# A graph layer on one core: an early small read of the adjacency, and half a tile rounded on VectorE in place of ScalarE

## The reference

```python
h   = maximum(layernorm(x, axis=-1), 0.0)     # (x - mean) / sqrt(var + 1e-5), no gain or offset
agg = matmul(adj, h)
out = x + relu(matmul(agg, W.T) + b)
```

## Time and profile before

| | |
|---|---|
| median of 3 runs | 381.19 us |
| the profiled execution's own time | 380.8 us |
| its span (first to last instruction) | 379.0 us |
| PE busy | 375.1 us (99%) |
| PE matmuls of the adjacency (L421) | 1536, each 389 ns on average, overlapping |
| DVE busy | 212.2 us (56%) |
| ACT busy | 181.8 us (48%) |
| POOL busy | 50.1 us (13%) |

### The profile page before, as it was taken

The page is one execution under the profiler, slowest core; times in us unless marked ns, Lnnn a source line. Parts: engine busy times, 40 slices in busy tenths (PEclk is TensorE's granted clock), DMA queues, the critical chain, the costliest instruction groups (busy, mean ns, idle before and its releaser), DMA issues.

```text
span 379.0 us, 4516 instructions
## 1 busy us (share of the span) xinstructions
PE 375.1 (99%) x1651; PEld 308.1 (81%) x1651; DVE 212.2 (56%) x294; ACT 181.8 (48%) x228; POOL 50.1 (13%) x88
## 2 busy tenths in 40 slices
PE   8999999999999999999999999999999999999997
PEld 4888888888888888888888888888888888888885
DVE  5999988874744453535564544444464444444424
ACT  5888776764443434343643343433355243434341
POOL 5687732320010000000001000000000100000000
PEclk9999999999999999999999999999999999999999
DMA  7989877577659565655566856565656775555203
GB/s 263 369 301 304 275 256 258 185 235 256 210 186 317 174 215 178 208 177 209 176 206 207 294 178 209 178 205 184 201 189 195 256 242 195 187 202 185 92 2 111
DMA packets 22774, 80.25 MB, mean 212 GB/s; under 512 B 2496, under 2 KB 2880, under 8 KB 22752
## 3 DMA queue, kind: packets, MB, share of 16 engines
q1 hardware_dynamic: 19584, 68.30, 54.1%
q0 software_dynamic: 3168, 11.67, 8.6%
HBM read 75.76 MB, written 4.19 MB: 211 GB/s over the span
## 4 chain that ended last, share of the span: by engine, by line
PE 98%; DMA 1%; DVE 0%; ACT 0%; POOL 0%; issue 0%; POOLq 0%
PE bank L421 92%; PE bank L463 6%; DMA x_sb<-x_dram 1%; ACT adj_hi L346 0%; POOL rstd L204 0%; ACT h_sb L352 0%; DVE out_sb L320 0%; DVE stats L240 0%; DVE mean_var L245 0%; DVE var_eps L249 0%; POOLq L200 0%
## 5 line engine op out<-in xcount | busy, mean ns | idle before, releaser
L421 PE MATMUL bank<-adj_hi,h_sb 128*128 128x512 f32 x1024 | 254.3, 389 | 0.2 <-ACT adj_hi L346 0.2
L229 DVE TENSOR_TENSOR adj_lo<-adj_in,adj_hi 128x1024 fp32r<-128x1024 f32 x126 | 154.6, 1227 | 145.7 <-ACT adj_hi L342 145.5
L421 PEld LDWEIGHTS bank<-adj_hi,h_sb 128*128 128x128 f32 x1024 | 192.0, 188 | 40.5 <-issue 0.5
L342 ACT ACTIVATE adj_hi<-adj_in 128x1024 fp32r<-128x1024 f32 x126 | 133.5, 1060 | 176.7 <-PE bank L421 174.5
L421 PE MATMUL bank<-adj_lo,h_sb 128*128 128x512 f32 x512 | 137.5, 389 | 0.0
L421 PEld LDWEIGHTS bank<-adj_lo,h_sb 128*128 128x128 f32 x512 | 96.1, 188 | 20.0
L204 POOL TENSOR_TENSOR rstd<-var_eps,minus_half 128x1 f32<-128x1 f32 x32 | 30.5, 954 | 3.4 <-DVE var_eps L249 0.8
L221 POOL DMA_DIRECT2D out_t_dram<-out_sb x3 | 2.2, 726 | 211.0 <-DVE out_sb L320 211.0
L352 ACT ACTIVATE h_sb<-centred,rstd 128x256 fp32r<-128x256 f32 x32 | 16.0, 499 | 3.6 <-POOL rstd L204 3.2
L362 ACT ACTIVATE centred<-x_sb,neg_mean 128x256 f32<-128x256 f32 x31 | 15.5, 500 | 2.1 <-DVE neg_mean L264 1.9
L270 DVE SCALAR_TENSOR_TENSOR h_sb<-centred,rstd,h_sb 128x256 fp32r<-128x256 f32 x32 | 15.3, 477 | 1.0 <-ACT h_sb L352 1.0
(11 more groups left out here) (25 smaller groups left out, 42.7 us busy)
## 6 DMA issues: line engine op xcount, KB each, us to landing
adj_in<-adj_t_dram SPq DMA_DIRECT2D x126, 512.0 KB, 3.6
xt_sb<-x_t_dram POOLq DMA_DIRECT2D x4, 1024.0 KB, 7.4
x_sb<-x_dram POOLq DMA_DIRECT2D x7, 512.0 KB, 6.5
out_t_dram<-out_sb POOLq DMA_DIRECT2D x3, 1024.0 KB, 4.9
adj_in<-adj_t_dram SPq DMA_DIRECT2D x4, 256.0 KB, 4.8
out_t_dram<-out_sb SPq DMA_DIRECT2D x3, 256.0 KB, 2.0
x_sb<-x_dram POOLq DMA_DIRECT2D x3, 128.0 KB, 4.6
w_sb<-w_t_dram POOLq DMA_DIRECT2D x1, 256.0 KB, 6.0
```

The costliest lines, as they stand in the source:

```text
L229: nc.vector.tensor_tensor(adj_lo[:, k, :], adj_in[:, k, :], adj_hi[:, k, :].bitcast(fp32), ALU.subtract).then_inc(s_lo, 1)
L342: nc.scalar.activation(adj_hi[:, k, :], adj_in[:, k, :], ACT.Copy).then_inc(s_hi, 1)
L421: last = nc.tensor.matmul(bank(g, kb, c)[:], h_sb[:, t, hp, kb * P:(kb + 1) * P], adj_parts[ap][:, n % U, chunk(c)], start=(t == 0 and (hp ...
```

## The change

ScalarE's queue issues, as the very first thing, a DMA of 16 columns of every fourth partition's row of adjacency tile 0 (32 rows of 64 bytes, rows 2 MB apart in memory) into a small tile `touched`, which nobody reads. SyncE waits for its landing only ahead of the last stores. VectorE rounds chunk 0 of tile 0 with a copy, between centre_first and h_rest(0), and waits for that chunk's landing itself. ScalarE no longer does this rounding; it waits until the count of rounded pieces is 1 before it rounds chunk 1. `WARM_ON` goes from 3 to 1.

```diff
-    WARM_ON = 3
+    WARM_ON = 1
...
+    TOUCH = 4
+    TOUCH_COLS = 16
...
+        touched = sb("touched", [P // TOUCH, TOUCH_COLS])
...
+        s_touched = sem("touched_landed")
...
+            sp.wait_ge(s_touched, 16)
             sp.wait_ge(s_out, 16 * LAST)
...
+            def first_rounded():
+
+                dve.wait_ge(s_early[0][0], 16)
+                nc.vector.tensor_copy(adj_hi[:, 0, chunk(0)], adj_in[:, 0, chunk(0)]).then_inc(s_hi, 1)
+
...
             centre_first()
+            first_rounded()
             h_rest(0)
...
+            act.dma_start(touched[:], adj_v[0:P:TOUCH, 0, 0:TOUCH_COLS]).then_inc(s_touched, 16)
+
             nc.scalar.activation(scratch[:], nc.const_aps.tensor(1.0, [P, 1], fp32), ACT.Copy)
             h_rounded(0)
-            early_rounded(0, 0)
+
+            act.wait_ge(s_hi, 1)
             early_rounded(0, 1)
```

## The result

The changed kernel takes 381.55 us (median of 21 runs, 380.89 to 382.84) against 381.1 us of the kernel before beside it (21 runs, 380.58 to 381.66). The ratio is 1.0015 with a 95% interval of 1.0008 to 1.0022: 0.3 to 0.8 us slower, small but real. The runs of the changed kernel also lie wider: four of the 21 stand between 382.75 and 382.84, where the kernel before has none; I call these the far runs. The profiled execution took 381.1 us, its span is 379.3.

What follows compares the result with a forecast made beforehand. TensorE is busy 375.1 of 379.0 us, so only its start at 5.84 could move. Starting 0.37 sooner, given back by tile 1, leaves +0.09 (381.28), or -0.05 with a fast copy; forecast 381.2, range 380.6 to 381.8.

Steps and rivals of the forecast that it cites:

- my likeliest case: Whole kernel: TensorE starts 0.37 us sooner, given back at chunk 1 and tile 1; -0.05 to +0.1 us in all, chance 0.42.
- The early read, δ = 0.44: Chunk 0's landing: the read brings it 0.44 us forward, to 4.63; 0 and -0.28 (a delay) kept as alternatives.
- the early read does nothing: Rival at chunk 0's landing: no help or a delay, VectorE pushed; time 381.5 to 382.0 us, chance 0.24.
- a push on VectorE: VectorE's queue behind the copy: h_rest(0) to h_rest(1) run later; 0.14 us in the forecast case, 0.41 or 0.67 before deductions in the rival.
- x held up: Rival at x's tile 0: served behind the read, x lands up to 0.42 us later; time 381.6, chance 0.11.
- The copy's duration: VectorE's rounding of chunk 0, 512 columns: 0.67 us taken, 0.41 and 0.71 kept as lower and upper ends.
- The gain at the start is given back: TensorE's first tiles: start 0.37 us sooner, lost again at chunk 1 and tile 1's low part of h, ending at +0.09.
- The first place: TensorE's fifth matmul: reached at 6.43, it waits up to 0.38 us for chunk 1, ready at 6.81.
- The second: Tile 1's third matmul: VectorE's low part of h ready at 9.26 instead of 9.17, 0.09 us later, setting the end.
- The shorter warm-up costs nothing: TensorE ahead of its start: two matmuls less free it at about 5.2 instead of 5.45, nothing on the path.
- The clock: Rival at tiles 0 and 1: less warm-up leaves TensorE at its lower level, +4.8 us, 386; chance 0.03.
- SyncE's wait and the later table load: SyncE's wait before the last stores and ScalarE's table load moved to end at 2.44: both cost nothing.

## Why the prediction was right, and where its steps were not

The number was close: 381.2 with a range of 380.6 to 381.8, and "within 0.2%" at 0.89; measured 381.55, a ratio of 1.0015. But it moved to the slower side, and my likeliest case was not the one that came: the number came close because every term at the beginning is small beside 381 us, which is luck as far as the mechanism goes. By its steps:

- *The early read, δ = 0.44*: wrong, and it is the step that decided. I took the slow 1.8 us at the beginning for a first access that can be had over with. The read made it slower: chunk 0 was 0.29 later in the changed kernel, and 0.2 to 0.6 later in the others with this read. Its lower end, -0.28, fits the 0.29 of the changed kernel by number, but was meant for 32 extra packets wherever they read; such packets out of x or tile 16 delayed x and not chunk 0. The time is that of the rival "the early read does nothing", which I gave 0.24, with its price of +0.27 to +0.53 and 0.28 more with a delay. Its start is right to the hundredth: with the delay of 0.28, its copy ends at 5.79 and TensorE starts at 5.93. Its path behind the start is not: it priced a push on VectorE, but h_rest(1) ended at 9.28 (8.81 + 0.47) and tile 1's third matmul stood at 9.07 + 2 x 0.23 = 9.53 without waiting for it. What decided was that chunk 1 landed late as well, for which it had no term. The rule of the Trainium skill that I set there ("DMA: Bandwidth & Descriptors", Issuing engines are not separate DMA queues: issuing from several engines only saves issue time) gives no price for this delay; the trace agrees only in that nothing was gained.
- *x held up*: happened (3.34 for 2.95), by 32 short packets and not by the second issue; a row alone does nothing. Its price of +0.42 was too much: with x late by 0.2 to 0.3 and chunk 0 in time, two kernels show 0.9999 and 1.0003.
- *The copy's duration*: 0.43 us, not the 0.67 that I took from the nearest row, and beside the lower end of 0.41. L255, with two per-partition operands, was a bad neighbour for a plain copy. By the Trainium skill ("VectorE: DVE Perf Modes", Mode 2×_2P) the copy goes at two elements a cycle, and this row agrees: 512 columns took about what L255 took for 256.
- *The gain at the start is given back*: right as far as the times go, and seen in the rounding alone (in the kernel without the read half of it remained): start 0.46 sooner, a wait at the fifth matmul until 6.64 (I had 6.81), tile 2 at 11.52 for 11.45. I forecast +0.09 from it, the trace says +0.07, and the runs can't tell it from nothing. The first place, chunk 1, is as I had it. The second is not: h of tile 1 was late by GpSimd's 0.74 us and not by a push on VectorE, which was idle there, so the near agreement of +0.09 and +0.07 is chance.
- *The shorter warm-up costs nothing*: right alone (1.0000). *The clock* was low at the first matmuls of the profiled execution, but chunk 1 was late by as much behind them, and with the clock high there tile 1 started no sooner (9.14). Nor was it this edit's doing: putting the matmuls back left the time as it was. Whether the far runs at 382.8 are the same thing at a larger size stays open.
- *SyncE's wait and the later table load*: nothing, as forecast.

## What to carry to other kernels

When two conditions become true in the same tenth of a microsecond, moving work off one of them gains only if the other can be moved too, and the next buffer to land then sets the end. A slow first transfer is not by itself a thing that a small read ahead can warm up; check this with the read alone before building on it, and above all if it reads the very rows that the real transfer reads next. When two delays end at the same moment, a profile shows only that both are there; take one away in a further kernel before naming a cause. Split such a bundle into its parts: here two of the three did nothing that could be measured.

## What the runs showed of the hardware

In one profile of each kernel: thirty-two reads of 64 bytes issued beside a load of 128 KB delay that load by 0.2 to 0.4 us (taken up at 3.14 to 3.34 for 2.95), 128 by 0.8, one or eight such reads don't. With a read of 32 or 128 of the rows that a transfer of 256 KB, issued about 0.4 us later, reads as well, that transfer is taken up at 5.27 to 5.72 instead of 4.67 to 5.11. A DMA issue that stands behind an activation on ScalarE's queue goes out at 0.80 us, while the activation runs only at 2.03. After the same ten warm-up matmuls TensorE was at its higher level by 5.09 us in the kernel before and not yet at 5.93 in the changed one.
